# One graph network kernel: the block sort counts all masks first and adds ranks on TensorE, two index tables are built in one stage, record scatters are spread anew

## The reference

```
x = norm(x + mean over edges of x[dst] summed to src, then a 2-layer MLP)   # _L0
x = norm(x + attention over edges src -> dst, with edge features, MLP)       # _L1
x = norm(x + (x + 3 * segment_sum(weight * x[dst], src)) / 4)                # _L2
x = norm(x + segment_sum(ht[type, src] + b[type], dst)
           + segment_sum(ht[type + 9, dst] + b[type + 9], src))              # _L3
```

## Time and profile before

| | us |
|---|---|
| median of 3 runs (5442.43 to 5445.99) | 5444.95 |
| the profiled execution's own time | 5444.79 |
| its span, first to last instruction | 5443.0 |

### The profile page before, as it was taken

One profiled execution on the slowest core, in us unless ns is written; L12 is line 12 of the kernel. 1 busy time (PEld: TensorE's weight loads), 2 busy tenths in 40 slices (PEclk: granted clock), 3 DMA queues, 4 the chain that ended last, 5 costly groups with the idle time before them and its releaser, 6 DMA issues. The chain is left out here.

```text
span 5443.0 us, 56992 instructions
## 1 busy us (share of the span) xinstructions
PE 2800.3 (51%) x13330; PEld 2304.1 (42%) x13331; DVE 2380.8 (44%) x3403; ACT 486.2 (9%) x765; POOL 3678.0 (68%) x3586
## 2 busy tenths in 40 slices
PE   1169999845555555525664873333333333333333
PEld 1158888832333333314554842333333333333332
DVE  6589998623555555556776054111111111111111
ACT  0035555000000000000001000000000000000000
POOL 0068888876777777774442755777777777777775
PEclk9999999867777777767877986555555665555555
DMA  4135555714888888844441843222222222221222
GB/s 128 32 92 135 133 131 138 273 33 109 216 216 220 217 216 219 215 125 114 120 118 50 294 163 110 53 53 53 53 53 53 53 49 53 53 53 53 53 53 53
DMA packets 692133, 626.43 MB, mean 115 GB/s; under 512 B 205815, under 2 KB 592037, under 8 KB 688357
## 3 DMA queue, kind: packets, MB, share of 16 engines
q1 hardware_dynamic: 455461, 294.10, 19.6%
q0 software_dynamic: 118496, 222.54, 16.0%
q10 hardware_dynamic: 118112, 109.05, 6.1%
HBM read 447.90 MB, written 190.20 MB: 117 GB/s over the span
## 5 line engine op out<-in xcount | busy, mean ns | idle before, releaser
L823 PE MATMUL ps<-g_got,g_hot 128*128 128x128 f32 x3264 | 759.3, 427 | 1295.3 <-DMA g_got<-y,s_msg 648.0
L585 POOL DMA_INDIRECT rec_by_src<-rec,pos x782 | 1070.2, 1368 | 431.7 <-issue 244.3
L823 PEld LDWEIGHTS ps<-g_got,g_hot 128*128 128x128 f32 x3264 | 705.2, 328 | 1349.5 <-issue 1349.5
L794 POOL DMA_INDIRECT g_got<-y,d_msg x816 | 769.8, 943 | 259.4 <-issue 248.4
L794 POOL DMA_INDIRECT g_got<-y,s_msg x816 | 769.8, 943 | 257.2 <-issue 248.4
L1091 POOL DMA_INDIRECT sc_kv<-kv,sc_cur x816 | 786.7, 964 | 220.3 <-issue 196.5
L647 PE MATMUL ps<-ln_low,ln_hot 128*125 128x256 f32 x2848 | 617.3, 380 | 11.3 <-DVE ln_low L624 11.3
L647 PEld LDWEIGHTS ps<-ln_low,ln_hot 128*125 128x125 f32 x2848 | 536.4, 188 | 92.1 <-issue 11.5
L807 DVE TENSOR_TENSOR g_hot<-ps,src_loc 128x1024 f32<-128x1024 f32 x102 | 124.5, 1224 | 840.7 <-PE ps L823 840.4
L807 DVE TENSOR_TENSOR g_hot<-ps,dst_loc 128x1024 f32<-128x1024 f32 x102 | 124.5, 1224 | 837.8 <-PE ps L823 837.5
L1142 DVE TENSOR_TENSOR sc_kve<-sc_kv,ps 128x1024 f32<-128x1024 f32 x204 | 249.2, 1221 | 395.7 <-DMA sc_kv<-kv,sc_cur 220.3
(11 more groups left out here) (277 smaller groups left out, 2529.3 us busy)
## 6 DMA issues: line engine op xcount, KB each, us to landing
linked<-ln_out SPq DMA_DIRECT2D x320, 224.0 KB
sc_locb<-loc SPq DMA_DIRECT2D x204, 256.0 KB, 3.7
ve<-sc_kve ACTq DMA_DIRECT2D x204, 256.0 KB, 5.0
wv_ve<-ve SPq DMA_DIRECT2D x102, 512.0 KB, 4.0
l_links<-linked SPq DMA_DIRECT2D x50, 800.0 KB, 6.8
l_links<-linked ACTq DMA_DIRECT2D x50, 800.0 KB, 8.7
y<-ms_y SPq DMA_DIRECT2D x25, 1152.0 KB
sc_attr<-attr SPq DMA_DIRECT2D x816, 16.0 KB
```

What stands on the lines that cost most here:

```text
L585: pool.indirect_dma_start(out=dram["rec_by_src"], out_offset=bass.IndirectOffsetOnAxis(ap=S["pos"][:, c:c + 1], axis=0), in_=S["rec"][:, c ...
L794: pool.indirect_dma_start(out=got[:, q, j, :], out_offset=None, in_=table, in_offset=bass.IndirectOffsetOnAxis(ap=index[:, c:c + 1], axis= ...
L823: last = pe.matmul(ps[:, bass.ds(columns[j], width)], hot[:, q, j, :], got[:, q, j, 0:width], start=False, stop=True, skip_group_check=True)
```

## The change

The sort becomes a function of its own, `sort_by_block`, with no loop register: 25 compares that count as they go (`accum_out`), two small matmuls for all 25 counts at once, then for each block a scan that starts at the block's first place, and a product with the mask. TensorE adds the 25 products in PSUM with an identity as weights.

```
-                link(dve.tensor_scalar(below[:, :], climb[:, :], limit[:, c:c + 1], None, ALU.is_lt))
-                link(dve.tensor_reduce(count[:, c:c + 1], below[:, :], AX.X, ALU.add))
+                    link(dve.tensor_scalar(below[:, :], s.climb[:, :], s.limit[:, c:c + 1], 0.0, ALU.is_lt, ALU.add,
+                                           accum_out=s.count[:, c:c + 1]))
...
+            for k, s in enumerate(stairs):
+                pool.wait_ge(tiled, k + 1)
+                pool.nop(nofuse=True)
+                for c in range(s.blocks):
+                    pool.indirect_dma_start(out=s.rows[:, c, :], out_offset=None, in_=whole,
+                                            in_offset=bass.IndirectOffsetOnAxis(ap=s.tile_i[:, c:c + 1], axis=0)).then_inc(got[k], 16)
+            if send is not None:
+                send_records(pool, S, dram, send)
...
+            for k, s in enumerate(stairs):
+                climb_of(s, k)
+            for k, s in enumerate(stairs):
+                dve.wait_ge(flipped, k + 1)
+                dve.tensor_copy(s.turned_columns[:, :], S["ps"][0:s.steps_of, (3 + 4 * k) * BANK:(3 + 4 * k) * BANK + P]).then_inc(listed, 1)
+            n = 0
+            for k, s in enumerate(stairs):
+                dve.wait_ge(got[k], 16 * s.blocks)
...
+                    if n >= 2:
+                        dve.wait_ge(turned, n - 1)
+                        if s.stored and n - 2 == sum(len(t.outputs) for t in stairs[:k]):
+                            dve.wait_ge(saved, 32)
...
+                    if what == "local" and s.stored:
+                        link(dve.tensor_copy(s.nodes[:, :].rearrange("p (b e) -> p b e", e=P), f[:, :, :, node_field]))
```

```
-RECORD_PARTS = {"link": 320, "l0": 105, "m0": 30, "project": 45, "maxima": 60, "l2": 105, "messages": 0}
+RECORD_PARTS = {"index": 10, "link": 300, "l0": 76, "m0": 36, "project": 48, "maxima": 72, "m1": 45, "l2": 100, "messages": 0}
...
-    pool.wait_ge(sent, 16 * (last - first))
+    if last == TILES:
+        pool.wait_ge(S["sent"], 16 * TILES)
...
-            sort_by_key(nc, S, "bysrc", 0, BLOCKS, 7)
+            sort_by_block(nc, S)
             store_records(nc, S, dram, "out")
-            staircase(nc, S, dram, "dst", P, PAIR_BLOCKS, 1, dram["rec_by_dst"],
-                      [(S["dst_loc"], "local"), (None, "node"), (S["d_src"], "source"), (S["d_msg"], "message")])
...
-                staircase(nc, S, dram, "win", NODES, W_BLOCKS, 1, dram["rec_by_dst"],
-                          [(S["win_lo"], "low"), (S["win_key"], "key"), (S["win_w"], "weight")])
+                index_stage(nc, S, dram, "ix", 1, dram["rec_by_dst"],
+                            [("win", NODES, W_BLOCKS, [(S["win_lo"], "low"), (S["win_key"], "key"), (S["win_w"], "weight")]),
+                             ("dst", P, PAIR_BLOCKS, [(S["dst_loc"], "local"), (S["d_src"], "source"), (S["d_msg"], "message")], True)],
+                            send="index")
...
-        staircase(nc, S, dram, "src", P, PAIR_BLOCKS, 0, dram["rec_by_src"], [(S["src_loc"], "local"), (S["s_msg"], "back")])
+        index_stage(nc, S, dram, "ixs", 0, dram["rec_by_src"],
+                    [("src", P, PAIR_BLOCKS, [(S["src_loc"], "local"), (S["s_msg"], "back")])])
```

More of the change, by code:

```diff
@@ L404, in staircase, with index_stage @@
+def index_stage(nc, S, dram, tag, node_field, records, specs, send=None):
     with ExitStack() as stack:
         m = Memory(nc, stack)
[L406 to L419, removed]
@@ L430, in staircase @@
-        order, built, turned, kept, stored = (m.sem(name + n) for n in ("_order", "_built", "_turned", "_kept", "_stored"))
-        moved = [k for k, (array, what) in enumerate(outputs) if what != "node"]
+        stairs = [Stair(m, S, *spec) for spec in specs]
+        widest = max(s.cols for s in stairs)
+        wide = m.sb(tag + "_wide", [P, 2, widest])
+        firsts = m.sb(tag + "_firsts", [1, TILES])
+        below = m.sb(tag + "_below", [P, TILES])
+        ready, fetched, spread, tiled, stepped, flipped, listed = (m.sem(tag + n) for n in (
+            "_iota", "_fetched", "_spread", "_tiled", "_stepped", "_flipped", "_listed"))
@@ L432, in staircase, with turn_of @@
+        got = [m.sem(f"{tag}_got{k}") for k in range(len(stairs))]
+        order, built, turned, kept, filed, saved = (m.sem(tag + n) for n in (
+            "_order", "_built", "_turned", "_kept", "_filed", "_saved"))
+        outputs = [(s, array, what) for s in stairs for array, what in s.outputs]
+        iotas = sum(4 if s.windows else 3 for s in stairs)
         block = stack.enter_context(nc.Block())
-        def turn_of(n):
+        def turn_of(n, cols):
             return S["ps"][:, (n % 2) * 4 * BANK:(n % 2) * 4 * BANK + cols]
@@ L480, in _ @@
             link = Chain(dve, order)
-            dve.wait_ge(spread, 1)
-            dve.wait_ge(ready, 4)
-            if windows:
-                link(dve.tensor_scalar_mul(held[:, 0:SPLIT_BLOCKS], split[:, :], float(per)))
-                for c in range(SPLIT_BLOCKS):
-                    link(dve.tensor_scalar(below[:, :], S["ps"][:, 0:TILES], held[:, c:c + 1], None, ALU.is_lt))
-                    link(dve.tensor_reduce(count[:, pair_blocks + c:pair_blocks + c + 1], below[:, :], AX.X, ALU.add))
@@ L488, in _ @@
-            link(dve.tensor_tensor(climb[:, :], climb[:, :], S["ps"][:, 0:TILES], ALU.add))
-            for c in range(pair_blocks):
-                link(dve.tensor_scalar(below[:, :], climb[:, :], limit[:, c:c + 1], None, ALU.is_lt))
-                link(dve.tensor_reduce(count[:, c:c + 1], below[:, :], AX.X, ALU.add))
-            link(dve.tensor_scalar(tile[:, :], count[:, 0:pair_blocks], 1.0, 1.0, ALU.max, ALU.subtract))
-            dve.tensor_copy(tile_i[:, :], tile[:, :]).then_inc(tiled, 1)
@@ L574, in _ @@
         def _(act):
[L575 to L581 removed]
+            for n, (s, array, what) in enumerate(outputs):
+                act.wait_ge(turned, n + 1)
+                act.activation(array[:, :], turn_of(n, s.cols), ACT.Copy).then_inc(kept, 1)
+            act.wait_ge(kept, len(outputs))
@@ L583, in send_records @@
+def send_records(pool, S, dram, stage):
     first, last = part_of(stage)
@@ L921, in _ @@
                 dve.wait_ge(normed, c + 1)
-        if first:
-            @block.gpsimd
-            def _(pool):
-                send_records(pool, S, dram, tag, sent)
+        @block.gpsimd
+        def _(pool):
+            send_records(pool, S, dram, tag)
         @block.tensor
```

279 lines of the change are left out of this document (156 added, 123 removed).

## The result

| | before | after |
|---|---|---|
| median, us | 5445.47 (4 runs, 5442.43 to 5446.81) | 5259.23 (4 runs, 5256.12 to 5261.54) |
| profiled execution, us | 5444.79 | 5256.12 |
| its span | 5443.0 | 5254.3 |

The ratio is 0.9658, interval 0.9642 to 0.9675. The time falls by 186 us; 172.5 were forecast.

A forecast was written before the change was run, and what follows sets the result against it. No single engine bounds the kernel, so each stage was asked by itself. Savings of 70 (sort), 43 (index), 3.9 (src) and 55.6 (scatters) make 172.5: span 5443.0 to 5270.5, time 5272 us, range 5246 to 5300.

The forecast's parts named there:

- The sort: Load and sort: counting compares, two count matmuls and 25 blocks at 2.70 us sum to 95.0; saves 70 us, bounds 60 to 82.
- the signs: Trace readings listed beforehand as showing it right or wrong, such as sort about 98 us and who is last at DRAINs.
- The first rival: In the sort and staircases, the counting compare keeps the fast rate: 5251 us in all, chance 0.14.
- The index stage: Two staircases of 117.3 us joined into one stage of 74.3, bounds 62 and 80; saves 43 us.
- link: Link stage with 300 scatters: GpSimd done near 943, SP last at 954.4; saves 15.0 us.
- maxima: Maxima stage with 72 scatters: GpSimd ends at 2479.3 against ScalarE's 2464.6; loses 14 us, bounds 0 and 18.
- l0: Stage l0 with 76 scatters: GpSimd ends at 1144.7, still behind VectorE's 1127.9; saves 38.9 us.
- messages: Messages stage with 95 scatters: GpSimd ends at 3304, SP last at 3307.4; saves 16.7 us.
- Link at the 1.2 GHz level: Rival: the new sort's TensorE work gets link granted the 1.2 GHz level; 5889 us, slower than before, chance 0.02.
- GpSimd late in more places than maxima: Rival: GpSimd also late in index (6 us), m1 (7) and project (3 more); 5288 us, chance 0.19.
- Scatters and joining give everything back: Rival: scatter parts return their gain and the merged index stage runs as two; about 5370 us, chance 0.02.
- The bounds: Whole kernel: the bounds of the unknown terms alone were said to give 5250 to 5292 us.

The follow-up runs named there:

- e2: The changed kernel with the old sort loop, everything else as changed: 6183.41 us, 69.4 above e4.
- e5: The changed kernel with plain compares in the sort and one reduce over all 25 masks for the counts: 5275.46 us, 9.4 above e8.
- e4: The changed kernel with a wait for scatter landings at the end of every stage's part: 6113.98 us, ratio 0.9706 to the kernel before on this chip.
- e6: The changed kernel with the sort's 25 products of mask and rank moved from VectorE to GpSimd: 5282.68 us, 16.6 above e8.
- e8: The changed kernel run again without edits: 5266.06 us, ratio 0.9664 to the kernel before.
- e10: The changed kernel with 60 scatters in maxima instead of 72, and 112 in l2: 5250.51 us, ratio 0.9646.
- e11: The changed kernel with e7's buffer and scatters rebalanced (index 0, link 305, l0 66, maxima 62, l2 113, n2 10, messages 97): 5234.58 us, ratio 0.9616.
- e7: The changed kernel with a third buffer for the message output and the index stage's 10 scatters moved to link (310): 5264.28 us.
- e12: e11 with ScalarE counting the first 12 masks of the sort and 112 scatters in l2: 5228.65 us, ratio 0.9604.
- e9: The changed kernel with the scatters shared out as before, as in e1, on another chip: 5314.60 us, ratio 0.9766.
- e1: The changed kernel with the scatters shared out over the stages as before, still without waits for landings: 6148.46 us, 34.5 above e4.
- e3: The changed kernel with dst and win in two index stages one after the other: 6165.64 us, 51.7 above e4.
- the first four runs: e1, e2, e3 and e4, run on a chip on which the kernel before took 6295.66 us.

## Why the prediction was right, step by step

- The sort: 70 predicted, 68.8 found, 69.5 by e2. The compare was 0.95 predicted and 0.89 found (1.5 us better in all). The block step was 2.70 predicted and 2.765 found (1.6 worse): the scan, which now starts from a column, is 1.84 where it was 1.79. The last TensorE pair was 1.4 predicted, 1.74 found. The load ahead of it was 0.6 longer, which was not foreseen. The "sort about 98 us" among the signs does not follow from the sum, which has 170.2 - 70 = 100.2 for the stage; it was 100.7.
- The first rival (0.14), that the counting compare keeps the fast rate, falls: it has 0.89, and by e5 the plain one has 0.48 in the same place.
- The index stage: 43 predicted, 42.0 found. The first steps came early, tile numbers at 25.0 for 26.1 and win's records at 44.3 for 45.2. The message output came late, at 68.5 for 67.1, and the stage's end too, 75.0 for 74.3. GpSimd was last by 1.5 (ScalarE 205.1, GpSimd 206.7). That gathers and scatters are held beside VectorE's build (up to 2.67 each, where 1.26 is the free pace) was in the estimate; but 74.3 itself was chosen between 72.1 and the 76 to 80 for a held GpSimd, and no row gave it.
- link 15.0 and 15.6, src 3.9 and 4.2, with the engine last that was named. maxima: 14 lost predicted, 12.8 found. GpSimd is last there as said; it ended 112.7 from the stage's start, and the sum's 2479.3 is 114.6. That sum gives 14.7 behind ScalarE, which was entered as 14.
- l0: 38.9 predicted, 44.4 found. The DRAIN's price and who is last were right. Two terms were mis-sized. The end of the 76th scatter, 167.7 from the stage's start, was taken from one execution. The six profiles of the changed kernel and its variants in which l0 sends 76 on the ordinary chips have 163.1 to 167.9 (163.6 in the profile of the result, 167.9 in e5), so it moves by 5 us from one execution to the next. That is 4.1 of the 5.5. The 1.3 for landing is the rest: without a wait it does not stand in front of the DRAIN, as e4 shows. GpSimd is last by 11.6 and not by the 17 of the signs.
- messages: 16.7 predicted, 22.3 found. SP was to be last, with its end read as fixed at 136.0 from the stage's start. In the profile of the result it ended at 129.5 and GpSimd was last, at 130.4; this sign came out wrong. In the nine profiles of the changed kernel and its variants on the ordinary chips SP's end is 129.5 to 136.4. SP is last in five of them (e5, e6, e8, e10, e11). In the other four GpSimd is: by under 1 us in the result, e7 and e12, and by 17 in e9, which sends 117. So the term was right for an execution in which SP ends near 136, and the lowest of the nine is the profile of the result.
- weigh: 0 predicted, 7.4 found, and nothing of the change is in it. In the thirteen profiles of the changed kernel and its variants it is 458.9 to 466.2; the one profile of the kernel before, 469.1, is 3 above all of them. e9, with the old parts, has 460.8, so it is not the scatters. Whether the kernel before is always that long stays open, as it was profiled once.
- The other rivals did not come. Link at the 1.2 GHz level (0.02): the granted clock stayed 1.00 in link's middle, also on the chip of e1 to e4. GpSimd late in more places than maxima (0.19): in index, where the sum had it, and in messages by 0.9; in m0, project and m1 it ended 2.1, 3.0 and 1.0 before the last engine. Scatters and joining give everything back (0.02): they are worth 55.4 (e9) and 31.6 (e3).
- The bounds: the distances from each term to its bounds, added up, give 42 us below 5272 and 32 above, 5230 to 5304. The recorded 5250 to 5292 is narrower, and how it was got is not said.

Between the two profiles 16.2 us more were saved than the sum had, and the median is 12.8 below the 5272. The surplus is 7.4 in weigh, 5.6 in messages and 5.5 in l0, with some small ones (maxima 1.2, m1 0.7, link 0.6); against them stand losses (project 1.5, sort 1.2, l2 1.1, index 1.0). So the mechanism came out stage by stage, but for who is last in messages. Luck has a part in both directions: in the sort the compare's 1.5 and the block step's 1.6 cancel, and the largest part of the surplus is in weigh, which the change does not touch. That l0's and messages' surplus is mostly the execution's own is argued and not shown. For it: over medians the new parts are worth 55.4 (e9), close to the 55.6 of the sum, and e8 has SP's end in messages at 136.3.

## What to carry to other kernels

Read who ends last at each barrier, and who is next. That difference, and not the work removed, is what a stage can give. Work that is spread over stages to fill a side engine has a price per piece at the barrier (0.08 us a scatter here) as well as in the queue (1.26). Fill each stage only up to several us below the engine that bounds it, because the fillers' pace (l0) and the stage's own end (messages) moved by 5 to 7 us between executions here. A count fused into a VectorE compare nearly doubled its time and was still half the price of a separate reduce. An idle ScalarE counted beside VectorE at no cost to it; an idle GpSimd gained nothing by multiplying beside VectorE's scans.

## What the runs showed of the hardware that was not expected

- GpSimd's DRAIN cost 0.082 to 0.083 us for each scatter of its stage, with or without a wait ahead of it. A count that begins anew after each 113 fits: 112 scatters gave 9.2, 113 gave 9.3, 117 gave 0.4, 310 (84 left) 6.9 and 320 (94 left) 7.7. No run sent 114 to 116. With few scatters and no wait the price does not show: behind the 10 of n2 (e11) the DRAIN ended 1.6 later, where 10 times 0.083 is 0.8.
- On the chip of the first four runs engines were idle for long stretches, without a wait that the profile shows, while GpSimd went on. In m1 of e4 its 45 scatters kept their 1.3 us pace. TensorE's last matmul ended at 3150.3; the VectorE instruction that adds the bias to its result started only at 3170.2, just when GpSimd's DRAIN had ended (3170.0). The stage was 94.6 long:

```profile
3147.83 2.50 PE L1020 MATMUL ps<-m_aggT,w_l 128*128 128x320 f32 x4 [4.28 <-ACT m_aggT L1036]
...
3170.18 0.82 DVE L990 TENSOR_TENSOR m_t<-ps,b_row 128x640 f32<-128x640 f32 x1 [30.52 <-remote]
```

m1 was 94.6, 82.9 and 91.1 with 45 scatters there (e4, e2, e3) and 66.1 without (e1). On the other chips it was 65.3 (e9) and 66.0 (before) without and 65.8 to 66.8 with them. In l2 of e4 the same shows within one stage. Windows while GpSimd scatters and from the end of its DRAIN on, in the columns of the earlier trace rows:

```profile
3240.00:3338.00 98.00, 13.39 (x36) 10.37 (x36) 0.00 (x0) 0.00 (x0) 67.02 (x70) 0.50 0.03 2
3338.00:3400.00 62.00, 59.42 (x501) 58.88 (x502) 0.00 (x0) 0.00 (x0) 0.00 (x0) 0.93 0.76 270
```

TensorE ran 36 matmuls in 98 us beside the scatters and 501 in the 62 us behind them, and the DMA engines were busy for 3% of those 98 us, so it was not their bandwidth. This fits indirect DMAs of GpSimd that hold up the other engines on such a chip; why they would is not known. Link and maxima, which send scatters too, were not longer there in e2 to e4 (635.0 to 636.0 and 112.1 to 113.8). In e4 the change was worth 2.9% on this chip, against 3.4% in the result and in e8.
